# One-hot row lists of a mixture-of-experts kernel: eight assignments per VectorE instruction, token numbers multiplied in by ScalarE

## The chip, the cores and the metric

The kernel runs on one core of a Trainium2 chip. The metric is the device time of one execution in microseconds. The profile follows the five engines of the core: PE (TensorE; PEld is its weight load), DVE (VectorE), ACT (ScalarE), POOL (GpSimd) and SP (SyncE, which only issues transfers).

## The reference, cut to what matters

Two layers are computed: cross attention and a dense FFN with spline-made weights, then a state-space block and a mixture of experts. The change lies in how the rows for the experts are listed. The part of the reference that it serves is this:

```python
x2d = hidden_states.reshape(T, D)                       # T = 2048 tokens, D = 512
router_logits = x2d @ gate_kernel                       # 32 experts
routing_weights = jax.nn.softmax(router_logits, axis=-1)
routing_weights, selected_experts = jax.lax.top_k(routing_weights, TOP_K)   # TOP_K = 8
...
flat_experts = selected_experts.reshape(-1)
sort_idx = jnp.argsort(flat_experts)
token_rows = sort_idx // TOP_K
sorted_inputs = jnp.take(x2d, token_rows, axis=0)
group_sizes = jnp.bincount(flat_experts, length=NUM_EXPERTS)
w0 = jax.lax.ragged_dot(sorted_inputs, gate_proj, group_sizes)
...
```

So the 2048 x 8 assignments have to be put in order of their expert, and for each tile of 128 sorted rows the kernel needs the 128 token numbers, to gather the rows.

## The kernel before

Four blocks follow one another, with all engines meeting between two of them. `block_a` and `block_b` hold attention, FFN and state space (up to about 818 us of the profiled execution). `block_c` finishes the layer (`gate`, `add`, `normal`), computes the router's logits, chooses eight experts for each token and makes the row lists. `block_d` gathers rows by these lists, tile by tile, and runs the experts; its first gather reads `idx_all`, the last thing that `block_c` writes on VectorE (L1520).

**Making the lists.** VectorE computes in `top_place` the place of each assignment in the sorted order: 128 tokens on the partitions, 16 token tiles (`NT`), eight assignments (`TOPK`). A place is split into `sf` (its slot within a row tile, 0 to 127) and `tf` (the number of its row tile). Then a scatter is done as a product of one-hots, in the loop over `t in range(NT)` at L1498:

- VectorE writes `hot_s[t % 2][:, k, :]`, 128 columns for each assignment k: is the column the slot `sf`, times the token's number `tok` (L1503). It writes `hot_t` for k = 0 and 1: is the column at least `tf`, 170 columns (`NSTEP`, L1505).
- ScalarE writes `hot_t` for k = 2 to 7, as a Sign with the bias `neg_tf` (L1602). Because Sign gives -1 and 1 and not 0 and 1, the first two assignments use doubled token numbers (`tok[:, 1]`), and the sum is halved at the end (L1518).
- TensorE multiplies for each k `hot_s` (stationary) by `hot_t` (moving, 170 columns), all 128 products adding up in `bank[4]` (L1693). Differences of neighbouring columns give the token numbers of each row tile (L1516 to L1520).

Both one-hots have two buffers, so writing tile t waits until TensorE has used tile t - 2 (`hot_used`). In both, the columns of one assignment are neighbours in memory.

**What runs beside it.** GpSimd computes the loop's control words (`meta`) with 25 small dependent steps on one partition from L1327 on. Earlier in `block_c` it splits the first expert's weights (L1316, L1319) while VectorE runs `gate(2)` and `gate(3)` (L1441, one instruction of 2048 columns with two inputs in SBUF each). The order on each engine is the order of the code; nothing is scheduled.

Of the kernel before, what the change touches and what calls it, by code (L numbers as in the profile page):

```python
# [34 lines left out]
NE, M, TOPK = 32, 192, 8  # L35
# [13 lines left out]
NMETA = NTILE + UNROLL  # L49
NSTEP = NMETA + 2  # L50
# [1143 lines left out]
def block_c(nc, a, X, ident, kept, bank, meta, idx_all, W, y0_d, y1_d, rows_d, joined):  # L1194

    with ExitStack() as s:
        sb, sem = mem(nc, s, "C")
        st, mv, rstd, shift = sb("st", [P, LT, 6]), sb("mv", [P, LT, 2]), sb("rstd", [P, LT]), sb("shift", [P, LT])
        st2, mv2, rstd2, shift2 = sb("st2", [P, NT, 6]), sb("mv2", [P, NT, 2]), sb("rstd2", [P, NT]), sb("shift2", [P, NT])
        spare = [t[:, 2:4, :].rearrange("p s n -> p (s n)").bitcast(F32) for t in (W.gu_hi, W.gu_lo)]  # L1200
# [3 lines left out]
        HOT_END = LT * L + TOPK * NSTEP // 2  # L1204
        hot_t = [t[:, LT * L:HOT_END].bitcast(F16).rearrange("p (k n) -> p k n", k=TOPK) for t in spare]
        tau, past = (spare[0][0:NE, HOT_END + n * NMETA:HOT_END + (n + 1) * NMETA] for n in range(2))
# [7 lines left out]
        pad, tok, padm, tok_id = sb("pad", [P, D]), sb("tok", [P, 2, NT]), sb("padm", [P, NMETA]), sb("tok_id", [P, NT + PADS], I32)  # L1214
        neg_tf, twice = sb("neg_tf", [P, NT * TOPK]), sb("twice", [P, NMETA])
        guess, part = sb("guess", [P, LT]), sb("part", [P, LT])
# [7 lines left out]
        slot_i, slot_s, slot_t = (sb(n, [P, NT * TOPK], I32) for n in ("slot_i", "slot_s", "slot_t"))  # L1224
        sf, tf = sb("sf", [P, NT * TOPK]), sb("tf", [P, NT * TOPK])
        hot_s = [sb(f"hot_s{i}", [P, TOPK, P], F16) for i in range(2)]

        HOT_V = 2
        padded = sb("padded", [P, NMETA])
# [4 lines left out]
        ids_done, lgT_done = sem("ids_done"), sem("lgT_done")  # L1234
        slots_done, hot_a_done = sem("slots_done"), sem("hot_a_done")
        ld_y, ld_c = [sem(f"ld_y{i}") for i in range(2)], sem("ld_c")
# [69 lines left out]
        def _(g):  # L1306
# [53 lines left out]
        def _(v):  # L1360
# [133 lines left out]
            step(v.tensor_scalar(slot_t[:, :], slot_i[:, :], 7, None, ALU.logical_shift_right))  # L1494
            v.tensor_copy(sf[:, :], slot_s[:, :])
            step(v.tensor_copy(tf[:, :], slot_t[:, :]))
            v.tensor_scalar(neg_tf[:, :], slot_t[:, :], -1.0, 0.5, ALU.mult, ALU.add).then_inc(slots_done, 1)
            for t in range(NT):  # L1498
                if t >= 2:
                    v.wait_ge(hot_used, t - 1)  # L1500
                for k in range(TOPK):
                    j = t * TOPK + k
                    i = v.tensor_scalar(hot_s[t % 2][:, k, :], iota_s[:, :], sf[:, j:j + 1], tok[:, int(k < HOT_V), t:t + 1], ALU.is_equal, ALU.mult)  # L1503
                    if k < HOT_V:
                        v.tensor_scalar(hot_t[t % 2][:, k, :], iota_t[:, :], tf[:, j:j + 1], None, ALU.is_ge)  # L1505
                i.then_inc(hot_done, 1)
            v.wait_ge(meta_sb, 2)
# [9 lines left out]
            step(v.tensor_tensor(twice[:, :], bank[4][:, 1:NMETA + 1], padded[:, :], ALU.subtract))  # L1517
            v.tensor_scalar(halves, twice[:, :], 0.5, -1.0, ALU.mult, ALU.add)  # L1518
            step(v.scalar_tensor_tensor(out=padded[:, :], in0=twice[:, :], scalar=0.0, in1=padm[:, :], op0=ALU.is_equal, op1=ALU.mult))
# [3 lines left out]
        def _(act):  # L1523
# [621 lines left out]
```

## Time and profile before

| | |
|---|---|
| median of 3 runs | 1570.62 us (1565.63 to 1570.64) |
| span of the profiled execution | 1567.3 us |
| busy, of that span | PE 1435.0, DVE 1153.4, ACT 918.4, POOL 1062.3 us |
| `block_c` | about 818 to 930.8 us |
| loop of one-hots in it | 891.3 to 929.0 us |

The time of the profiled execution itself is not listed beside its span; the span lies among the three runs, 3.3 us under their median, so a difference worked out in the trace is put on the median. A line of the profile names the code line, the engine, the operation, output and inputs, and their shapes. `W_gu_hi` and `W_gu_lo` in the loop's rows are `hot_t`, which lies in spare room of the weight buffers; `W_d_hi` there are GpSimd's scratch rows.

### The profile page before, as it was taken

What the parts mean: (1) busy time and instruction counts of PE and PEld (TensorE: products, weight loads), DVE (VectorE), ACT (ScalarE), POOL (GpSimd) and SP (SyncE); (2) the same over time, 40 slices, a digit from 0 to 9 for tenths busy, and PEclk for the clock granted to TensorE, in tenths of its full rate; (3) what the DMA queues carried; (4) which work ended last, traced back from release to release, by engine and by line L of the source; (5) the groups of instructions that cost most, each with busy time, mean ns of one, the idle gap of its engine ahead of it and who ended that gap; (6) DMA issues with size and microseconds to landing.
All of it is one profiled execution on the core that took longest, in us unless ns stands there. A gap on an engine that the chain in (4) does not pass through costs nothing. (4 is left out here: it accounts for less than half of the span.)

```text
span 1567.3 us, 26498 instructions
## 1 busy us (share of the span) xinstructions
PE 1435.0 (92%) x6453; PEld 1073.9 (69%) x6454; DVE 1153.4 (74%) x2069; ACT 918.4 (59%) x1420; POOL 1062.3 (68%) x654
## 2 busy tenths in 40 slices
PE   6999878999999999999975559989999999999997
PEld 3444556666666666666644238878988888898886
DVE  5888897888888878888878786656666666565554
ACT  6777677666667666766646664444544444444442
POOL 2222287999999989999941235757666676666675
PEclk9999989999999999999988759999999999999999
DMA  8232557888899889988869416889998899888876
GB/s 314 96 111 98 180 132 144 179 197 205 192 196 217 186 195 178 221 188 195 176 150 336 159 31 159 193 193 209 198 200 192 191 206 201 203 186 190 189 146 118
DMA packets 106416, 283.95 MB, mean 181 GB/s; under 512 B 16641, under 2 KB 18850, under 8 KB 95090
## 3 DMA queue, kind: packets, MB, share of 16 engines
q0 software_dynamic: 43520, 155.57, 50.0%
q1 hardware_dynamic: 60322, 123.12, 26.4%
q10 hardware_dynamic: 2512, 4.52, 0.8%
q8 instruction: 27, 0.44, 0.1%
q14 instruction: 35, 0.29, 0.1%
HBM read 152.28 MB, written 135.08 MB: 183 GB/s over the span
## 5 line engine op out<-in xcount | busy, mean ns | idle before, releaser
L1156 POOL TENSOR_TENSOR B_E<-B_dtu,B_BC 128x512 f32<-128x512 f32 (+3 forms) x121 | 309.3, 2670 | 16.7 <-DMA B_BC<-bc_d 16.7
L2080 POOL DMA_INDIRECT out_x<-D_y,D_rows x144 | 243.8, 1693 | 75.4 <-issue 43.6
L889 ACT ACTIVATE bank<-B_dtv,negA 128x512 f32<-128x512 f32 x256 | 173.5, 690 | 159.8 <-DVE B_E L1024 98.1
L1024 DVE TENSOR_TENSOR_SCAN B_E<-bank,B_E 128x512 f32<-128x512 f32 x192 | 230.2, 1214 | 42.5 <-ACT bank L889 34.8
L1162 POOL TENSOR_TENSOR B_E<-B_E,B_BC 128x1536 f32<-128x1536 f32 x64 | 234.0, 3656 | 34.5 <-DVE B_E L1024 29.8
L2045 POOL DMA_INDIRECT D_rows<-rows_d,D_source x144 | 155.9, 1083 | 129.0 <-DMA out_x<-D_y,D_rows 62.3
L806 PE MATMUL bank<-B_Wd,B_inter 128*128 128x512 f32 x512 | 231.9, 606 | 9.0 <-DVE X L1011 5.3
L1906 ACT ACTIVATE D_xT_hi<-bank 128x512 fp32r<-128x512 f32 x147 | 88.1, 599 | 231.5 <-PE bank L1815 167.8
L1826 PE MATMUL bank<-W_gu_hi,D_xT_hi 128*128 x584 | 202.4, 347 | 14.5 <-ACT D_xT_hi L1906 13.9
L1968 DVE TENSOR_TENSOR D_xT_lo<-bank,D_xT_hi 128x512 fp32r<-128x512 f32 x147 | 101.3, 689 | 141.1 <-ACT D_xT_hi L1906 108.7
L1827 PE MATMUL bank<-W_gu_lo,D_xT_hi 128*128 x584 | 199.2, 341 | 0.0
L806 PEld LDWEIGHTS bank<-B_Wd,B_inter 128*128 128x128 f32 x512 | 98.3, 195 | 122.8 <-issue 102.8
L1832 PE MATMUL bank<-W_gu_hi,D_xT_lo 128*128 x584 | 131.8, 348 | 6.8 <-DVE D_xT_lo L1968 5.5
L1946 ACT ACTIVATE D_y<-bank 128x512 f32<-128x512 f32 x144 | 86.4, 600 | 83.2 <-PE bank L1899 63.6
L1826 PEld LDWEIGHTS bank<-W_gu_hi,D_xT_hi 128*128 128x128 f32 x584 | 111.1, 190 | 27.5 <-issue 22.2
L1832 PEld LDWEIGHTS bank<-W_gu_hi,D_xT_lo 128*128 128x128 f32 x584 | 103.3, 191 | 18.6 <-DVE D_xT_lo L1968 14.0
L1827 PEld LDWEIGHTS bank<-W_gu_lo,D_xT_hi 128*128 128x128 f32 x584 | 111.2, 190 | 5.5
L794 PE MATMUL bank<-hT_hi,B_Wg_hi 128*128 128x512 f32 x256 | 105.4, 412 | 7.3 <-DVE hT_lo L1064 7.3
L2032 DVE TENSOR_TENSOR W_gu_lo<-W_raw_gu,W_gu_hi x30 | 52.8, 1761 | 66.4 <-ACT W_gu_hi L1916 51.3
L795 PE MATMUL bank<-hT_lo,B_Wg_hi 128*128 128x512 f32 x256 | 100.8, 394 | 0.0
L796 PE MATMUL bank<-hT_hi,B_Wg_lo 128*128 128x512 f32 x256 | 100.3, 392 | 0.0
L1011 DVE TENSOR_TENSOR X<-bank,X 128x512 f32<-128x512 f32 x128 | 86.7, 678 | 18.2 <-PE bank L806 18.2
(327 smaller groups left out, 3263.7 us busy)
## 6 DMA issues: line engine op xcount, KB each, us to landing
y_d<-B_E POOLq DMA_DIRECT2D x64, 1024.0 KB, 10.7
B_BC<-bc_d SPq DMA_DIRECT2D x128, 256.0 KB, 6.2
W_raw_gu<-in_wgu SPq DMA_DIRECT2D x64, 384.0 KB
W_raw_d<-in_wd SPq DMA_DIRECT2D x64, 256.0 KB
X<-in_x SPq DMA_DIRECT2D x4, 1024.0 KB, 9.2
y_d<-A_du SPq DMA_DIRECT2D x4, 1024.0 KB, 4.0
dt_d<-A_dtv SPq DMA_DIRECT2D x4, 1024.0 KB, 3.9
dtu_d<-A_dtu SPq DMA_DIRECT2D x4, 1024.0 KB, 4.1
```

What stands on the lines that cost most here:

```text
L794: pe.matmul(ps[:, :], hi, h_hi, start=k == 0, stop=False)
L806: mm = pe.matmul(Yb[t % 2][:, :], chunk(jj, ch)[:, t * P:(t + 1) * P], Wd[w][:, ch, :], start=ch == 0, stop=ch == 1)
L889: act.activation(dA[m % 2][:, :], dtv[:, c, :], ACT.Exp, scale=negA[:, c, n:n + 1]).then_inc(dA_done, 1)
L1024: v.tensor_tensor_scan(state, dA[m % 2][:, :], E[:, s % NR, c, :], 0.0, ALU.mult, ALU.add).then_inc(s_done, 1)
L1156: g.tensor_tensor(E[:, s % NR, c:end, :], dtu[:, at:at + end - c, :], spread(BC[op % NBC][:, :], end - c), ALU.mult).then_inc(dbu_done, 1)
L1162: g.tensor_tensor(E[:, s % NR, 0:NW, :], E[:, s % NR, 0:NW, :], spread(BC[op % NBC][:, :], NW), ALU.mult).then_inc(prod_done, 1)
L1826: pe.matmul(ps, *operands(k, xT_hi, W.gu_hi), start=k == 0, stop=False)
L1827: pe.matmul(ps, *operands(k, xT_hi, W.gu_lo), start=False, stop=False)
L1832: mm = pe.matmul(ps, *operands(k, xT_lo, W.gu_hi), start=False, stop=k == KC - 1)
L1968: v.tensor_tensor(xT_lo[i % 2][:, :], pT[:, :], xT_hi[i % 2][:, :], ALU.subtract).then_inc(xT_sb, 1)
L2045: g.indirect_dma_start(rows[i], None, rows_d[:, :], bass.IndirectOffsetOnAxis(ap=source[i // HALF][:, i % HALF:i % HALF + 1].bitcast(U32), ...
L2080: g.indirect_dma_start(a["out"], bass.IndirectOffsetOnAxis(ap=rows[i][:, ROW - 1:ROW].bitcast(U32), axis=0), ysb[:, i, :], None, compute_o ...
```

## The change

The two one-hots of a token tile are laid out with the assignment innermost (`[P, n, k]`), and each is made by one VectorE instruction for all eight assignments: `is_equal` over 128 x 8 = 1024 columns and `is_ge` over 170 x 8 = 1360 columns, both with two fp16 inputs in SBUF. One input is a wide copy of the column numbers, each repeated eight times (`wide_s`, `wide_t`); the other is the eight values of `sf` or `tf`, read again for each column number. GpSimd makes the wide copies ahead of its weight split. ScalarE no longer makes tiles; it multiplies the slots by the token numbers, 1024 columns at once, from the new buffers `same` into `hot_s`. TensorE now reads both operands with a step of eight elements, 16 bytes. The doubling, the halving and `neg_tf` go.

```diff
-        hot_t = [t[:, LT * L:HOT_END].bitcast(F16).rearrange("p (k n) -> p k n", k=TOPK) for t in spare]
+        HOT_V = TOPK
+        hot_t = [t[:, LT * L:HOT_END].bitcast(F16) for t in spare]
+        hot_tv = [t[:, 0:HOT_V * NSTEP].rearrange("p (n k) -> p n k", k=HOT_V) for t in hot_t]
...
-        sf, tf = sb("sf", [P, NT * TOPK]), sb("tf", [P, NT * TOPK])
-        hot_s = [sb(f"hot_s{i}", [P, TOPK, P], F16) for i in range(2)]
-
-        HOT_V = 2
+        sf, tf = (sb(n, [P, NT, TOPK], F16) for n in ("sf", "tf"))
+        hot_s = [sb(f"hot_s{i}", [P, P, TOPK], F16) for i in range(2)]
+        free = [z[i].rearrange("p t l -> p (t l)").bitcast(F16) for i in range(2)]
+        wide_s = free[0][:, 0:P * TOPK].rearrange("p (n k) -> p n k", k=TOPK)
+        wide_t = free[0][:, P * TOPK:P * TOPK + NSTEP * HOT_V].rearrange("p (n k) -> p n k", k=HOT_V)
+        same = [free[1][:, i * P * TOPK:(i + 1) * P * TOPK].rearrange("p (n k) -> p n k", k=TOPK) for i in range(2)]
...
             g.wait_ge(x2_done, LT + 1)
+            g.tensor_copy(wide_s[:, :, :], each(iota_s[:, :], P, TOPK))
+            g.tensor_copy(wide_t[:, :, :], each(iota_t[:, :], NSTEP, HOT_V)).then_inc(ids_done, 1)
             g.tensor_tensor(W.slot(W.gu_lo, 0), W.slot(W.raw_gu, 0), W.slot(W.gu_hi, 0), ALU.subtract).then_inc(W.gu_split, 1)
...
-            v.tensor_scalar(neg_tf[:, :], slot_t[:, :], -1.0, 0.5, ALU.mult, ALU.add).then_inc(slots_done, 1)
+            v.wait_ge(ids_done, 2)
...
             for t in range(NT):
                 if t >= 2:
+                    v.wait_ge(hot_a_done, t - 1)
+                v.tensor_tensor(same[t % 2][:, :, :], wide_s[:, :, :], over(sf[:, t, :], P), ALU.is_equal).then_inc(same_done, 1)
+                if t >= 2:
                     v.wait_ge(hot_used, t - 1)
-                for k in range(TOPK):
-                    j = t * TOPK + k
-                    i = v.tensor_scalar(hot_s[t % 2][:, k, :], iota_s[:, :], sf[:, j:j + 1], tok[:, int(k < HOT_V), t:t + 1], ALU.is_equal, ALU.mult)
-                    if k < HOT_V:
-                        v.tensor_scalar(hot_t[t % 2][:, k, :], iota_t[:, :], tf[:, j:j + 1], None, ALU.is_ge)
-                i.then_inc(hot_done, 1)
+                v.tensor_tensor(hot_tv[t % 2], wide_t[:, :, :], over(tf[:, t, :], NSTEP), ALU.is_ge).then_inc(hot_done, 1)
...
-            v.tensor_scalar(halves, twice[:, :], 0.5, -1.0, ALU.mult, ALU.add)
+            v.tensor_scalar(halves, twice[:, :], -1.0, None, ALU.add)
...
-            act.wait_ge(slots_done, 1)
             for t in range(NT):
                 if t >= 2:
                     act.wait_ge(hot_used, t - 1)
-                for k in range(HOT_V, TOPK):
-                    j = t * TOPK + k
-                    i = act.activation(hot_t[t % 2][:, k, :], iota_t[:, :], ACT.Sign, bias=neg_tf[:, j:j + 1])
-                i.then_inc(hot_a_done, 1)
+                act.wait_ge(same_done, t + 1)
+                act.activation(hot_s[t % 2][:, :, :], same[t % 2][:, :, :], ACT.Copy, scale=tok[:, 0, t:t + 1]).then_inc(hot_a_done, 1)
...
-                    mm = pe.matmul(bank[4][:, 0:NSTEP], hot_s[t % 2][:, k, :], hot_t[t % 2][:, k, :],
+                    mm = pe.matmul(bank[4][:, 0:NSTEP], hot_s[t % 2][:, :, k], hot_tv[t % 2][:, :, k],
```

On VectorE the loop begins so before the change:

```order
L1496 CAST C_tf<-C_slot_t 128x128
L1497 TENSOR_SCALAR C_neg_tf<-C_slot_t 128x128
L1503 TENSOR_SCALAR C_hot_s<-C_iota_s,C_sf,C_tok 128x128
L1505 TENSOR_SCALAR W_gu_hi<-C_iota_t,C_tf 128x170
L1503 TENSOR_SCALAR C_hot_s<-C_iota_s,C_sf,C_tok 128x128
L1505 TENSOR_SCALAR W_gu_hi<-C_iota_t,C_tf 128x170
L1503 TENSOR_SCALAR C_hot_s<-C_iota_s,C_sf,C_tok 128x128 x7
L1505 TENSOR_SCALAR W_gu_lo<-C_iota_t,C_tf 128x170
```

And so after it, where `C_z` is the room of the buffers `wide_s`, `wide_t` and `same`:

```order
L1503 TENSOR_SCALAR C_slot_t<-C_slot_i 128x128
L1504 CAST C_sf<-C_slot_s 128x128
L1505 CAST C_tf<-C_slot_t 128x128
L1514 TENSOR_TENSOR C_z<-C_z,C_sf 128x1024
L1517 TENSOR_TENSOR W_gu_hi<-C_z,C_tf 128x1360
L1514 TENSOR_TENSOR C_z<-C_z,C_sf 128x1024
L1517 TENSOR_TENSOR W_gu_lo<-C_z,C_tf 128x1360
```

Ten instructions per token tile have become two, and the two are wide. On GpSimd, between the copy of the token numbers and the metadata steps, before:

```order
L1311 DMA y_d<-y_d 128x2048
L1313 COPY C_share<-C_tok_id 128x20
L1316 TENSOR_TENSOR W_gu_lo<-W_raw_gu,W_gu_hi 128x1536
L1319 TENSOR_TENSOR W_d_lo<-W_raw_d,W_d_hi 128x1024
L1327 TENSOR_TENSOR W_d_hi<-W_gu_lo,W_d_hi 1x168
```

And after:

```order
L1317 COPY C_share<-C_tok_id 128x20
L1323 COPY C_z<-C_iota_s 128x1024
L1324 COPY C_z<-C_iota_t 128x1360
L1325 TENSOR_TENSOR W_gu_lo<-W_raw_gu,W_gu_hi 128x1536
L1328 TENSOR_TENSOR W_d_lo<-W_raw_d,W_d_hi 128x1024
L1336 TENSOR_TENSOR W_d_hi<-W_gu_lo,W_d_hi 1x168
```

Two copies stand ahead of the weight split now.

## Rows read from the trace of the kernel before

**Rows 1.** Timeline, end of the loop and of `block_c`: start us, us, engine, line

```profile
927.49 0.23 DVE L1508 CAST W_d_hi<-W_d_hi 1x168 int32<-1x168 f32 x1
927.70 1.32 PE L1693 MATMUL bank<-W_gu_lo,C_hot_s 128*128 128x170 f16 x8 [0.82 <-DVE C_hot_s L1503]
...
929.12 0.33 DVE L1516 COPY C_padded<-bank 128x168 f32<-128x168 f32 x1
...
930.38 0.33 DVE L1520 TENSOR_TENSOR idx_all<-C_place,C_padded 128x168 int32<-128x168 f32 x1
```

**Rows 2.** Windows of the loop: stretch, its us, busy us of each engine, PEclk

```profile
889.00:907.00 18.00, 7.17 (x45) 5.54 (x46) 17.86 (x79) 14.60 (x44) 15.30 (x25) 0.50 0.19 71
907.00:927.50 20.50, 12.52 (x77) 9.18 (x75) 20.50 (x98) 18.91 (x55) 0.00 (x0) 0.50 0.00 0
```

**Rows 3.** Waits from 889 to 931 us: us in total, times, longest

```profile
PE bank L1693 <- DVE C_hot_s L1503: 19.1, 16, 4.8
```

**Rows 4.** Timeline, first slots, and starts of PE on a tile

```profile
891.16 0.23 DVE L1497 TENSOR_SCALAR C_neg_tf<-C_slot_t 128x128 f32<-128x128 int32 x1
...
893.73 1.29 PE L1693 MATMUL bank<-W_gu_hi,C_hot_s 128*128 128x170 f16 x8 [4.79 <-DVE C_hot_s L1503]
...
908.51 1.32 PE L1693 MATMUL bank<-W_gu_hi,C_hot_s 128*128 128x170 f16 x8 [0.82 <-DVE C_hot_s L1503]
...
910.64 1.31 PE L1693 MATMUL bank<-W_gu_lo,C_hot_s 128*128 128x170 f16 x8 [0.81 <-DVE C_hot_s L1503]
```

**Rows 5.** Groups from 889 to 931 us: busy us, mean ns of one

```profile
L1693 PE MATMUL bank<-W_gu_hi,C_hot_s 128*128 128x170 f16 x64 | 10.5, 344 | 11.5 <-DVE C_hot_s L1503 11.5
```

**Rows 6.** Timeline, VectorE with two float32 inputs

```profile
827.39 2.29 DVE L1441 TENSOR_TENSOR C_z<-W_gu_lo,C_z 128x2048 f32<-128x2048 f32 x1
829.60 2.48 DVE L1394 TENSOR_TENSOR X<-bank,X 128x512 f32<-128x512 f32 x4
```

**Rows 7.** Timeline, ScalarE: two widths of Copy, and one with two pointers

```profile
832.57 1.49 ACT L1526 ACTIVATE W_gu_hi<-W_raw_gu 128x1536 fp32r<-128x1536 f32 x1 [1.66 <-DMA W_raw_d<-in_wd]
...
833.96 0.61 ACT L1716 ACTIVATE W_d_hi<-W_raw_d 128x512 fp32r<-128x512 f32 x1
...
843.40 2.94 ACT L1547 ACTIVATE C_row<-X,C_shift,C_rstd 128x512 f32<-128x512 f32 x4 [6.67 <-DVE C_shift L1411]
```

**Rows 8.** Timeline, GpSimd's L543: `A_table` read by neighbours

```profile
37.14 1.27 POOL L543 TENSOR_TENSOR A_taps<-A_taps,A_table 128x512 f32<-128x512 f32 x1 [6.92 <-DMA A_dtu<-in_powers]
```

**Rows 9.** The same line two instructions later: `A_table` read four floats apart

```profile
39.60 1.58 POOL L543 TENSOR_TENSOR A_taps<-A_taps,A_table 128x512 f32<-128x512 f32 x1
```

**Rows 10.** Timeline, PE with 384 float32r columns in neighbouring words

```profile
945.26 0.34 PE L1827 MATMUL bank<-W_gu_lo,D_xT_hi 128*128 x1
945.43 0.86 PE L1832 MATMUL bank<-W_gu_hi,D_xT_lo 128*128 x4
```

**Rows 11.** Timeline, GpSimd and VectorE at `gate(2)`

```profile
837.52 3.41 POOL L1316 TENSOR_TENSOR W_gu_lo<-W_raw_gu,W_gu_hi 128x1536 fp32r<-128x1536 f32 x1
840.00 3.08 DVE L1441 TENSOR_TENSOR W_d_lo<-W_gu_hi,W_d_lo 128x2048 f32<-128x2048 f32 x1 [2.55 <-DMA W_gu_hi<-y_d]
...
847.10 2.36 POOL L1319 TENSOR_TENSOR W_d_lo<-W_raw_d,W_d_hi 128x1024 fp32r<-128x1024 f32 x1 [6.17 <-DVE X L1394]
```

**Rows 12.** Timeline, start of `block_d`: VectorE and GpSimd

```profile
931.17 1.75 DVE L1971 TENSOR_TENSOR W_gu_lo<-W_raw_gu,W_gu_hi 128x1536 fp32r<-128x1536 f32 x1
...
931.73 2.18 POOL L2049 DMA_INDIRECT D_rows<-rows_d,idx_all  x1 [24.84 <-POOLq L1196]
932.84 1.22 DVE L1972 TENSOR_TENSOR W_d_lo<-W_raw_d,W_d_hi 128x1024 fp32r<-128x1024 f32 x1
934.22 0.98 POOL L2049 DMA_INDIRECT D_rows<-rows_d,idx_all  x1 [0.30 <-issue]
```

**Rows 13.** Timeline, first and last step of GpSimd's metadata

```profile
889.54 0.53 POOL L1327 TENSOR_TENSOR W_d_hi<-W_gu_lo,W_d_hi 1x168 f32<-1x168 f32 x1 [40.08 <-ACT W_d_hi L1595]
...
906.12 0.77 POOL L1356 TENSOR_SCALAR meta<-W_d_hi 1x168 int32<-1x168 f32 x1
```

More of the change, by code:

```diff
@@ L1214, in block_c @@
         pad, tok, padm, tok_id = sb("pad", [P, D]), sb("tok", [P, 2, NT]), sb("padm", [P, NMETA]), sb("tok_id", [P, NT + PADS], I32)
-        neg_tf, twice = sb("neg_tf", [P, NT * TOPK]), sb("twice", [P, NMETA])
+        twice = sb("twice", [P, NMETA])
         guess, part = sb("guess", [P, LT]), sb("part", [P, LT])
@@ L1234, in block_c @@
         ids_done, lgT_done = sem("ids_done"), sem("lgT_done")
-        slots_done, hot_a_done = sem("slots_done"), sem("hot_a_done")
+        hot_a_done, same_done = (sem(n) for n in ("hot_a_done", "same_done"))
         ld_y, ld_c = [sem(f"ld_y{i}") for i in range(2)], sem("ld_c")
@@ L1313, in _, with each @@
             g.tensor_copy(share[:, :, NE:NE + 1].bitcast(I32), tok_id[:, :].rearrange("p (t o) -> p t o", o=1)).then_inc(ids_done, 1)
+            def each(t, n, k):
+                return t.rearrange("p (n o) -> p n o", o=1).broadcast_to([P, n, k])
             g.wait_ge(W.gu_hi_done, 1)
             g.wait_ge(x2_done, LT + 1)
+            g.tensor_copy(wide_s[:, :, :], each(iota_s[:, :], P, TOPK))
+            g.tensor_copy(wide_t[:, :, :], each(iota_t[:, :], NSTEP, HOT_V)).then_inc(ids_done, 1)
             g.tensor_tensor(W.slot(W.gu_lo, 0), W.slot(W.raw_gu, 0), W.slot(W.gu_hi, 0), ALU.subtract).then_inc(W.gu_split, 1)
@@ L1494, in _, with over @@
             step(v.tensor_scalar(slot_t[:, :], slot_i[:, :], 7, None, ALU.logical_shift_right))
-            v.tensor_copy(sf[:, :], slot_s[:, :])
-            step(v.tensor_copy(tf[:, :], slot_t[:, :]))
-            v.tensor_scalar(neg_tf[:, :], slot_t[:, :], -1.0, 0.5, ALU.mult, ALU.add).then_inc(slots_done, 1)
+            v.tensor_copy(sf[:, :, :].rearrange("p t k -> p (t k)"), slot_s[:, :])
+            step(v.tensor_copy(tf[:, :, :].rearrange("p t k -> p (t k)"), slot_t[:, :]))
+            v.wait_ge(ids_done, 2)
+            def over(t, n):
+                return t.rearrange("p (o k) -> p o k", o=1).broadcast_to([P, n, t.shape[-1]])
             for t in range(NT):
                 if t >= 2:
+                    v.wait_ge(hot_a_done, t - 1)
+                v.tensor_tensor(same[t % 2][:, :, :], wide_s[:, :, :], over(sf[:, t, :], P), ALU.is_equal).then_inc(same_done, 1)
+                if t >= 2:
                     v.wait_ge(hot_used, t - 1)
-                for k in range(TOPK):
-                    j = t * TOPK + k
-                    i = v.tensor_scalar(hot_s[t % 2][:, k, :], iota_s[:, :], sf[:, j:j + 1], tok[:, int(k < HOT_V), t:t + 1], ALU.is_equal, ALU.mult)
-                    if k < HOT_V:
-                        v.tensor_scalar(hot_t[t % 2][:, k, :], iota_t[:, :], tf[:, j:j + 1], None, ALU.is_ge)
-                i.then_inc(hot_done, 1)
+                v.tensor_tensor(hot_tv[t % 2], wide_t[:, :, :], over(tf[:, t, :], NSTEP), ALU.is_ge).then_inc(hot_done, 1)
             v.wait_ge(meta_sb, 2)
```

## The prediction, made before the changed kernel ran

> **What bounds the kernel now.** The change touches one stretch, so I looked first for where it lies: the timeline puts the loop of one-hots between 891.3 and 929.0 us, 38 of 1567 us. Then I asked what its end holds up. VectorE's last reads of `bank[4]` start 0.1 us after TensorE's last product, the list `idx_all` is the last instruction of the block, and the next block starts 0.3 us behind it [rows 1]. Block D opens with gathers that need the list [rows 12], and its weight loads start only behind those, so a microsecond won or lost in this loop should move everything after it. The reader is to see that no transfer and no other engine ends later here: GpSimd's metadata chain is done at 906.9 us [rows 13].
>
> Next, what sets the loop's pace. In the windows VectorE is busy all 20.50 of 20.50 us, ScalarE 18.9, TensorE 12.5 [rows 2], and TensorE waits for `hot_s` of VectorE in 16 of 16 tiles, 19.1 us in all [rows 3]. So VectorE is the bound. From 910.64 to 927.70 us TensorE starts eight tiles, 2.13 us each; from 893.73 to 908.51 us six tiles, 2.46 us each [rows 1, 4]. The slower ones are those beside GpSimd's 25 steps, which take 17.4 us [rows 13], 0.69 us each, 3.5 to a tile: VectorE loses 0.33 us per tile, or 0.1 us per GpSimd step.
>
> TensorE works at a granted clock of 0.50, the 1.2 GHz level [rows 2]. Eight products take 1.32 us, one alone 0.344 [rows 1, 5], so they follow each other at (1.32 - 0.344) / 7 = 0.139 us, or 0.82 ns for each of 170 columns. A tile costs it 8 x 0.139 = 1.11 us and 0.2 us of latency.
>
> **Part 1, VectorE.** Removed: eight L1503 and two L1505 per tile, and L1497; the loop's first instruction can start where L1497 does now, at 891.16 us [rows 4]. Added per tile: one instruction of 1024 columns, one of 1360. Two float32 inputs go at one column per 1.04 ns and 0.08 us per instruction: 2048 columns, start to start, are 829.60 - 827.39 = 2.21 us, and four of 512 take 2.48 [rows 6]. At that rate a tile is 1.15 + 1.50 = 2.64 us, which is more than today's 2.13. The inputs are now fp16; were they read in pairs, it is 0.61 + 0.79 = 1.40 us. No row has two 2-byte inputs on VectorE. The two bounds are 1.40 and 2.64; I take 1.40, since the instructions of the loop now, also fp16, go faster than one column per 1.04 ns (ten instructions and 1364 columns in 2.13 us, fixed costs included [rows 4]). The other bound is a rival.
>
> The Trainium skill, "VectorE: DVE Perf Modes", section "The perf-mode tier table", lists `tensor_tensor` on bf16 in SBUF at twice the rate of fp32, and "Vector Engine (DVE) Microarchitecture Reference", section 5.1, has that hold also where a row is read again and again. By it the tile is 1.40 us, without it 2.64.
>
> **Part 2, ScalarE.** Six Sign instructions per tile become one Copy of 1024 columns. Copy takes 1.49 us for 1536 and 0.61 for 512 columns, 0.86 ns a column, and pointers add about 0.1 us (four with two pointers: 2.94 us) [rows 7]. So 0.61 + 0.44 + 0.1 = 1.15 us, less than a tile on VectorE. But it now stands in a row: `is_equal`, Copy, products. For the first tile that is 891.16 + 0.69 + 1.15 + 0.1 of semaphores = 893.1 us for TensorE's start, against 893.73 now. A ring Copy, products, next but one Copy costs 1.15 + 1.32 + 0.2 = 2.7 us per two tiles, under 2 x 1.40, so it isn't the pace as long as TensorE keeps its 1.32.
>
> **Part 3, TensorE.** Still 128 products, but both operands are read with a step of 16 bytes. Nothing in the trace has TensorE reading so. The bounds for a column:
> - 0.82 ns, no cost at all (the loop now).
> - 0.82 + 0.61 = 1.43 ns. GpSimd's L543 exists in two forms that differ in this step alone: `A_table` read by neighbours takes 1.27 us [rows 8], read four floats (16 bytes) apart 1.58 us [rows 9], 0.31 us for 512 elements.
> - 1.81 ns. TensorE's float32r products of 384 columns follow each other at (0.86 - 0.34) / 3 = 0.173 us [rows 10]; that is 96 pieces of 16 bytes, 1.81 ns each. If a piece is what it fetches at a time, and that is its fastest, a 16-byte step costs a piece per column.
> - 3.1 ns, the whole time of one element in the strided L543 (1.58 us / 512), as the far end.
>
> I take 1.5: the row with just this step, moved a little towards the row of TensorE itself. Then a product is 0.255 us, a tile 2.04, more than VectorE's 1.40: **TensorE becomes the bound**. 16 x 2.04 + 0.2 = 32.8 us from 893.1 ends at 925.9, against 929.02 now [rows 1]: **-3.1 us**. The weight loads have 128 columns with the same step against 170 and stay under the products.
>
> The Trainium skill speaks on both sides. "SBUF — State Buffer", section "Specifications (TRN2)", asks for at least two hits in each 16-byte line for full bandwidth, which a step of 16 bytes never has; under "Door 1: The DMA port swizzle" the same page lets one stride for free up to 8 bf16 elements, which is this step. By the first the cost is real, by the second TensorE stays at 1.32 us per tile and the first rival below holds.
>
> **Part 4, GpSimd's two copies.** They write 2384 columns ahead of its weight split L1316, beginning at about 837.6 us. Bounds: L1316 with two inputs costs 3.41 us for 1536, 2.2 ns a column [rows 11], so 5.3 us; half of that, with one input, 2.6 us. They end between 840.2 and 842.9. There `gate(2)` on VectorE starts at 840.00; it takes 3.08 us, where 2.29 is its time alone [rows 6, 11], because L1316 runs until 840.93. The other direction shows at 931.73, where GpSimd takes 2.18 us and not 0.98 while VectorE's pair instructions run [rows 12]: whichever runs holds the other until it ends. So `gate(2)` ends at 842.5 if it slips in behind short copies (-0.6), at 845.2 behind long ones (+2.1), at 845.9 if L1316 gets in first (+2.8). VectorE is nearly gapless after it, so this counts. L1316 comes later and its first reader is the load of expert 2, far behind; L1319 waits for `x2_done` anyway until 847.1. I take **+0.5 us**, nearer to the short copies.
>
> **Part 5, the rest.** The halving goes but its instruction stays. The new wait `ids_done` is met 45 us early. `hot_a_done` ahead of `is_equal` is met when Copy of t - 2 is done. 0 us.
>
> Sum: -3.1 + 0.5 = -2.6 us. On the median of 1570.62 that is **1568.0 us**. With 1.43 to 1.81 ns for a column this forecast's own range is 1566.5 to 1575.
>
> **Rival A, the step is free (or TensorE's clock rises and hides it).** VectorE sets the pace: 891.16 + 16 x 1.40 + 25 x 0.1 for GpSimd's steps = 916.0 us; TensorE ends at 917.7 and the block 11.3 us earlier. Against all of it speaks GpSimd: each of its 25 steps may now wait behind an instruction of 0.61 or 0.79 us; with half of 0.7 each the metadata ends at 915.7, with all of it at 924.4, later than VectorE's end at 919.4, and 6.3 us stay of the gain. 1559.3 to 1564.8, most likely 1560.6. The busy share of TensorE now, 12.5 of 20.5 us, left the clock low [rows 2]; a denser loop might raise it, which speaks for this rival.
>
> **Rival B, slower: the step costs much more.** The place is the same 21,760 columns. The change breaks even when they take what the loop has now, 929.02 - 893.1 - 0.2 = 35.7 us: **1.64 ns a column**. It is 0.5% slower from 2.0 ns. At 2.4, midway between 1.81 and 3.1, the loop lasts 52.4 us: +16.5 + 0.5, 1587.6 us. For it: if both operands, each with the step, share one way of reading. Against it: GpSimd, also with two streams, pays 0.61.
>
> **Rival C, slower: VectorE takes no pairs.** The change then doesn't do what it is made for. 891.16 + 42.3 + 2.5 = 935.9, TensorE 1.4 us later, 937.3: +8.3 + 0.5, 1579.4 us. Decides if a column costs more than 0.85 ns on VectorE.
>
> **Chances.** Forecast 0.45; A 0.30; B 0.12; C 0.08; the rest 0.05, collisions at `gate(2)` or a metadata chain that eats the gain, all within half a per cent. Half a per cent, 7.85 us, is about what a measurement of this kernel can tell from no change. A is over it in four fifths of its cases (0.24), the forecast where the column costs under 1.3 ns (0.03): faster 0.27. Slower: B and most of C, 0.18. Within: 0.55. The range: down to A's best case, 1558.5, and up over C, 1581; B and small remainders stay out.
>
> **What would show it.** TensorE's group L1693: eight products in 2.0 us, with an idle time before them near nothing, confirm part 3; 1.3 us or less is A, 3 us and more is B. VectorE's two groups: 0.69 and 0.87 us are pairs, 1.22 and 1.57 are not. GpSimd's metadata should end by 921 us and its two copies last 2.6 us; `gate(2)` should end by 843.6. The forecast is wrong if the step costs TensorE nothing, and also if the loop's gain doesn't reappear in the span.

## The result, and the profile after

The changed kernel takes 1573.84 us (median of 22 runs, 1566.77 to 1581.50), the kernel before beside it 1567.42 us (22 runs, 1557.97 to 1574.01). The ratio is 1.0044, 95% interval 1.0029 to 1.0060, and a second comparison gave 1.0044 again (1.0022 to 1.0067): **0.44% or 6.9 us slower**, where 2.6 us faster was forecast. The ratios are estimates over all runs and differ a little from the quotients of the medians, here 1.0041. The profiled execution took 1576.29 us, its span 1574.5.

The loop's second half on the windows view (stretch, its us, busy us of PE, PEld, DVE, ACT, POOL, then PEclk), against [rows 2]:

```profile
889.00:907.00 18.00, 12.64 (x42) 5.76 (x42) 15.23 (x39) 7.38 (x8) 13.43 (x18) 0.50 0.22 75
907.00:927.50 20.50, 20.50 (x68) 9.72 (x67) 12.78 (x17) 9.19 (x8) 6.09 (x8) 0.50 0.00 0
```

TensorE has no gap left, VectorE went from 20.50 to 12.78 us and ScalarE from 18.9 to 9.2. TensorE's granted clock is still 0.50: working without a pause did not raise it. The groups (busy us, mean ns of one, idle before) and the waits of the loop, against [rows 3, 5]:

```profile
L1701 PE MATMUL bank<-W_gu_hi,C_hot_s 128*128 128x170 f16 x64 | 21.0, 485 | 4.2 <-ACT C_hot_s L1611 4.2
L1611 ACT ACTIVATE C_hot_s<-C_z,C_tok 128x1024 f16<-128x1024 f16 x16 | 18.4, 1149 | 20.9 <-PE bank L1701 18.0 <-DVE C_z L1514 2.9
L1514 DVE TENSOR_TENSOR C_z<-C_z,C_sf 128x1024 f16<-128x1024 f16 x16 | 12.6, 787 | 0.0
L1517 DVE TENSOR_TENSOR W_gu_lo<-C_z,C_tf 128x1360 f16<-128x1360 f16 x8 | 7.3, 916 | 5.9 <-PE bank L1701 5.9
```

The waits have turned round: ScalarE waits for TensorE 18.0 us and VectorE 11.5, TensorE for ScalarE only once. On the timeline the pace and the end of the loop, against [rows 1, 4]:

```profile
893.73 0.69 DVE L1514 TENSOR_TENSOR C_z<-C_z,C_sf 128x1024 f16<-128x1024 f16 x1
...
905.52 2.63 PE L1701 MATMUL bank<-W_gu_hi,C_hot_s 128*128 128x170 f16 x8
907.97 2.62 PE L1701 MATMUL bank<-W_gu_lo,C_hot_s 128*128 128x170 f16 x8
...
932.40 2.62 PE L1701 MATMUL bank<-W_gu_lo,C_hot_s 128*128 128x170 f16 x8
935.13 0.33 DVE L1527 COPY C_padded<-bank 128x168 f32<-128x168 f32 x1 [2.68 <-PE bank L1701]
...
936.39 0.33 DVE L1531 TENSOR_TENSOR idx_all<-C_place,C_padded 128x168 int32<-128x168 f32 x1
```

A tile is (907.97 - 905.52) = 2.45 us, a product (2.62 - 0.485) / 7 = 0.305 us, **1.80 ns a column**. And where GpSimd's copies meet `gate(2)`, GpSimd's rows and then VectorE's, against [rows 11] (L1325 and L1450 are L1316 and L1441 of before):

```profile
836.56 1.03 POOL L1323 COPY C_z<-C_iota_s 128x1024 f16<-128x1024 f16 x1
837.54 1.32 POOL L1324 COPY C_z<-C_iota_t 128x1360 f16<-128x1360 f16 x1
838.82 5.47 POOL L1325 TENSOR_TENSOR W_gu_lo<-W_raw_gu,W_gu_hi 128x1536 fp32r<-128x1536 f32 x1
...
838.57 2.42 DVE L1450 TENSOR_TENSOR W_d_lo<-W_gu_hi,W_d_lo 128x2048 f32<-128x2048 f32 x1 [2.04 <-DMA W_gu_hi<-y_d]
840.92 0.17 DVE L1419 RECIPROCAL C_rstd<-C_rstd 128x4 f32<-128x4 f32 x1
841.12 3.19 DVE L1420 SCALAR_TENSOR_TENSOR C_shift<-C_mv,C_rstd 128x4 f32<-128x4 f32 x1
844.23 2.46 DVE L1408 BATCH_NORM_STATS2 C_st<-X 128x6 f32<-128x512 f32 x4
```

`gate(2)` slips in behind the short copies and ends early, as hoped. But L1325 has waited for it, gets in behind it, and L1420 on VectorE, an instruction of 0.16 us in the kernel before (there L1411), takes 3.19 us.

To compare traces that drift against each other, I cut `block_c` of each into three stretches on VectorE: from the block's first statistics to those behind `gate(2)`; from there to the loop's first instruction (in before, L1497); from there to `idx_all`. Each length runs from start to start, in us; each ratio is against before measured beside it:

| kernel | to behind gate(2) | to the loop | loop to idx_all | sum | ratio, 95% interval |
|---|---|---|---|---|---|
| before | 25.06 | 47.88 | 39.22 | 112.16 | |
| before, second trace | 25.14 | 49.50 | 39.21 | 113.85 | |
| changed | 26.91 | 49.50 | 42.66 | 119.07 | 1.0044, 1.0029 to 1.0060 |
| changed, second trace | 27.26 | 49.37 | 42.66 | 119.29 | 1.0044, 1.0022 to 1.0067 |
| copies late | 25.08 | 49.49 | 42.65 | 117.22 | 1.0008, 0.9984 to 1.0031 |
| step of 8 bytes | | | | | 0.9958, 0.9931 to 0.9984 |
| 8 bytes, copies late | 25.03 | 49.48 | 29.67 | 104.18 | 0.9945, 0.9919 to 0.9971 |
| the same again | 25.02 | 47.85 | 29.68 | 102.55 | 0.9945, 0.9926 to 0.9964 |
| 4 bytes, copies late | 25.04 | 47.86 | 29.25 | 102.15 | 0.9938, 0.9917 to 0.9958 |
| moving operand near | 27.30 | 47.85 | 40.28 | 115.43 | 1.0030, 0.9998 to 1.0062 |
| weights near | 27.27 | 49.45 | 43.43 | 120.15 | |

The loop costs +3.4 us, `gate(2)` +1.8 to 2.2. The middle stretch has two lengths, 1.6 us apart, taken up below. What follows `idx_all` can't be compared in single traces: from its start to the end of the span it is 636.9 and 644.5 us in the two traces of before, 638.1 and 630.6 us in the two of the changed kernel. That the block's loss comes back in the whole time rests on the ratios.

### The profile page after: what moved, and what is told of

It is laid out like the page before. It is cut to its first block and busy times, and to the rows that moved or that the text cites. A ratio compares the mean times of both kernels' runs of the same rounds, so it can differ in the third digit from the quotient of the medians.

```text
span 1574.5 us, 26306 instructions
## 1 busy us (share of the span) xinstructions
PE 1454.5 (92%) x6453; PEld 1079.9 (69%) x6454; DVE 1145.5 (73%) x1940; ACT 902.4 (57%) x1340; POOL 1063.7 (68%) x656
## 5 line engine op out<-in xcount | busy, mean ns | idle before, releaser
L2088 POOL DMA_INDIRECT out_x<-D_y,D_rows x144 | 237.7, 1651 | 84.3 <-issue 48.4
L1162 POOL TENSOR_TENSOR B_E<-B_E,B_BC 128x1536 f32<-128x1536 f32 x64 | 232.4, 3632 | 33.4 <-DVE B_E L1024 27.3
L794 PE MATMUL bank<-hT_hi,B_Wu_hi 128*128 128x512 f32 x256 | 99.8, 390 | 0.0
```

What stands on the lines that cost most here:

```text
L794: pe.matmul(ps[:, :], hi, h_hi, start=k == 0, stop=False)
L1162: g.tensor_tensor(E[:, s % NR, 0:NW, :], E[:, s % NR, 0:NW, :], spread(BC[op % NBC][:, :], NW), ALU.mult).then_inc(prod_done, 1)
L2088: g.indirect_dma_start(a["out"], bass.IndirectOffsetOnAxis(ap=rows[i][:, ROW - 1:ROW].bitcast(U32), axis=0), ysb[:, i, :], None, compute_o ...
```

## The experiments

**What a step costs TensorE.** Products of zeros in the kernel before, six groups. `spaced(n)` reads every n-th fp16 value as the moving operand, `far` is a stationary operand with a step of eight:

```diff
+            def spaced(n):
+                cols = halfs.rearrange("p (m n) -> p n m", n=n)
+                return cols[:, 0:2, 0:128] if n == 8 else cols[:, 0, 0:256]
...
+                near, far = before[:, :], halfs.rearrange("p (m n) -> p n m", n=8)[:, 0, :]
+                for i in range(16):
+                    pe.matmul(bank[5][:, 0:256], near, halfs[:, 0:256], start=True, stop=True)
+                for i in range(12):
+                    pe.matmul(bank[5][:, 0:256], near, spaced(2), start=True, stop=True)
...
+                for i in range(12):
+                    pe.matmul(bank[5][:, 0:256], far, spaced(8), start=True, stop=True)
```

> The kernel before with 76 products of zeros added twice, at the start of the router's logits and in the loop of one-hots ahead of tile 8; their sums go to a bank that is written over, so they change times alone. Each has 256 fp16 columns: 16 with both operands contiguous, 12 each with the moving operand at a step of 4, 8 and 16 bytes, 12 with the stationary alone at 16 bytes, 12 with both at 16. Theory 1 (16-byte pieces, one per 1.8 ns): 0.82, 0.82 and 0.9 ns a column for contiguous, 4 and 8 bytes, 1.8 ns at 16 bytes, that is 0.21, 0.21, 0.23 and 0.46 us a product; the stationary alone at 16 bytes costs 128 x 1.8 = 0.23 us for its load, hidden or nearly so under the product. Theory 2 (any step costs a whole fetch per element): 1.8 ns at every step. Theory 3 (the weight load is what became slow, and the products wait for it): the moving operand alone costs nothing at any step, the stationary alone gives 0.3 us a product as in the changed kernel. If the granted clock is higher at one of the two places, a cost in ns that stays the same is memory's, one that halves is TensorE's own.

PE's timeline at the first place (start, us of the group, line; in the order of the expectation):

```profile
857.69 1.92 PE L1670 MATMUL bank<-C_pad,C_before 128*128 128x256 f16 x16
859.45 1.52 PE L1672 MATMUL bank<-C_pad,C_before 128*128 128x256 f16 x12
860.81 2.88 PE L1674 MATMUL bank<-C_pad,C_before 128*128 128x256 f16 x12
863.51 5.60 PE L1676 MATMUL bank<-C_pad,C_before 128*128 128x256 f16 x12
868.93 2.74 PE L1678 MATMUL bank<-C_pad 128*128 128x256 f16 x12
871.47 5.68 PE L1680 MATMUL bank<-C_pad 128*128 128x256 f16 x12
```

The windows of the fourth group and of the fifth (PEclk is the third column from the end):

```profile
863.50:868.50 5.00, 5.00 (x13) 1.30 (x12) 0.00 (x0) 0.00 (x0) 0.00 (x0) 0.97 0.03 11
868.50:871.30 2.80, 2.80 (x14) 1.98 (x13) 0.00 (x0) 0.00 (x0) 0.00 (x0) 0.50 0.00 0
```

Start to start, a moving column costs 0.43 ns contiguous, 0.44 at 4 bytes, 0.88 at 8 and 1.77 at 16 (2.70, 5.42 us for twelve products of 256 columns). The stationary operand alone at 16 bytes gives 0.83 ns (2.54 us for twelve), what contiguous products cost at this clock [rows 1]; at the high clock it was not measured. Theory 1 holds and theory 3 falls: the moving operand pays, the weight load stays under the product. At a clock of 0.97 here and 0.50 in the changed loop 16 bytes cost the same, 1.77 and 1.80 ns, so this cost does not follow TensorE's clock; that it lies in fetching the operand is inferred from this. The second place gave the same durations at 8 and 16 bytes (2.88 and 5.60 us).

**Is it a piece of 16 bytes?**

```diff
+                    pe.matmul(bank[5][:, 0:256], before[:, :], spaced(3), start=True, stop=True)
...
+                    pe.matmul(bank[5][:, 0:256], before[:, :], spaced(32), start=True, stop=True)
```

> The kernel before with 60 products of zeros added at each of the two places of the first probe (their sums are written over): a contiguous stationary operand, 256 moving fp16 columns, 12 products each at a step of 2, 6, 12, 32 and 64 bytes. The first probe gave 0.44, 0.88 and 1.77 ns a column at 4, 8 and 16 bytes. Theory 1 (pieces of 16 bytes, each fetched once): 0.66 and 1.33 ns at 6 and 12 bytes, and 1.77 ns again at 32 and 64 bytes, since a column can't cost more than a piece of its own. Theory 2 (the operand is read through, every byte between the columns too, at 9 bytes per ns): 0.66 and 1.33 ns at 6 and 12 bytes, 3.5 ns at 32 and 7.1 ns at 64. Theory 3 (a step that divides 16 is special): 6 and 12 bytes cost 1.77 ns as well.

```profile
859.90 2.22 PE L1673 MATMUL bank<-C_pad,C_before 128*128 128x256 f16 x12
861.96 4.24 PE L1675 MATMUL bank<-C_pad,C_before 128*128 128x256 f16 x12
866.02 5.71 PE L1677 MATMUL bank<-C_pad,C_before 128*128 128x256 f16 x12
871.55 5.35 PE L1679 MATMUL bank<-C_pad,C_before 128*128 128x256 f16 x12
876.73 3.60 PE L1627 MATMUL bank<-ident,C_row 128*128 128x128 f32 x15
```

Start to start, 6 bytes cost 0.67 ns a column, 12 bytes 1.32, 32 bytes 1.80, 64 bytes 1.69. The cost grows with the step up to 16 bytes and stays there: that fits pieces of 16 bytes at 1.7 to 1.8 ns each, of which a column needs at most one. Theories 2 and 3 fall. And the cost is no surcharge on TensorE's own pace: at 16 bytes a column takes 1.77 ns where a contiguous one takes 0.43 and 1.80 where it takes 0.82. The slower of the two paces counts, not their sum.

**One operand near at a time, in the kernel itself.** First `hot_t` as before:

```diff
-        hot_tv = [t[:, 0:HOT_V * NSTEP].rearrange("p (n k) -> p n k", k=HOT_V) for t in hot_t]
+        hot_tv = [t[:, 0:HOT_V * NSTEP].rearrange("p (k n) -> p k n", k=HOT_V) for t in hot_t]
...
-                v.tensor_tensor(hot_tv[t % 2], wide_t[:, :, :], over(tf[:, t, :], NSTEP), ALU.is_ge).then_inc(hot_done, 1)
+                v.tensor_tensor(hot_tv[t % 2], wide_t[:, :, :], tf[:, t, :].rearrange("p (k o) -> p k o", o=1).broadcast_to([P, HOT_V, NSTEP]), ALU.is_ge).then_inc(hot_done, 1)
...
-                    mm = pe.matmul(bank[4][:, 0:NSTEP], hot_s[t % 2][:, :, k], hot_tv[t % 2][:, :, k],
+                    mm = pe.matmul(bank[4][:, 0:NSTEP], hot_s[t % 2][:, :, k], hot_tv[t % 2][:, k, :],
```

> The changed kernel with hot_t alone laid out as before, the columns of one assignment neighbours: TensorE's moving operand is contiguous, its stationary operand keeps the 16-byte step. VectorE's is_ge then reads each value of tf 170 times in a row. If the moving operand alone carries the cost of the step: eight products in 1.3 to 1.4 us for 2.62, 0.82 ns a column; the loop is then VectorE's. If VectorE takes such reads in pairs, is_ge stays at 0.87 us, the loop takes 28 us for 41 and the kernel is 12 us under the changed one, 4 to 6 us under the kernel before; if not, is_ge takes 1.50 us (1.04 ns a column), a tile 2.2 us and more beside GpSimd, the loop 38 to 40 us, and the kernel 1 to 3 us under the changed one, 4 to 6 us over the kernel before. If the stationary operand carries the cost, TensorE stays at 2.44 us per tile and nothing changes.

A tile late in the loop:

```profile
923.75 1.56 DVE L1517 TENSOR_TENSOR W_gu_hi<-C_z,C_tf 128x1360 f16<-128x1360 f16 x1
...
925.24 0.68 DVE L1514 TENSOR_TENSOR C_z<-C_z,C_sf 128x1024 f16<-128x1024 f16 x1
925.37 1.36 PE L1701 MATMUL bank<-W_gu_hi,C_hot_s 128*128 128x170 f16 x8 [0.73 <-DVE W_gu_hi L1517]
```

TensorE is back at 1.36 us, so the moving operand carried the cost. But `is_ge` lost its pairs, 1.56 us and not 0.87: a value read 170 times in a row is no pair. The time is 4.7 us over before (-0.3 to +9.8), as expected for this case. Now the reverse, `hot_s` near:

```diff
-        hot_s = [sb(f"hot_s{i}", [P, P, TOPK], F16) for i in range(2)]
+        hot_s = [sb(f"hot_s{i}", [P, TOPK, P], F16) for i in range(2)]
...
-                act.activation(hot_s[t % 2][:, :, :], same[t % 2][:, :, :], ACT.Copy, scale=tok[:, 0, t:t + 1]).then_inc(hot_a_done, 1)
+                act.activation(hot_s[t % 2][:, :, :], same[t % 2].rearrange("p n k -> p k n"), ACT.Copy, scale=tok[:, 0, t:t + 1]).then_inc(hot_a_done, 1)
...
-                    mm = pe.matmul(bank[4][:, 0:NSTEP], hot_s[t % 2][:, :, k], hot_tv[t % 2][:, :, k],
+                    mm = pe.matmul(bank[4][:, 0:NSTEP], hot_s[t % 2][:, k, :], hot_tv[t % 2][:, :, k],
```

> The reverse of the run with a contiguous moving operand: ScalarE writes hot_s with each assignment's slots as neighbours and reads same with the 16-byte step, so that TensorE's stationary operand is contiguous and the moving one keeps its step. If the moving operand alone carries the cost, TensorE stays at 2.44 us per tile (1.80 ns a column), with shorter weight loads (0.10 for 0.15 us) that buy nothing, and the time is the changed kernel's within 1 us, unless ScalarE pays for its own step: up to 1.8 ns a column would make Copy 1.15 into 1.9 us, still under TensorE's 2.44. If the stationary operand carries it, eight products take 1.3 us.

```profile
L1611 ACT ACTIVATE C_hot_s<-C_z,C_tok 128x1024 f16<-128x1024 f16 x16 | 33.9, 2128 | 7.1 <-PE bank L1701 4.7 <-DVE C_z L1514 2.4
L1701 PE MATMUL bank<-W_gu_lo,C_hot_s 128*128 128x170 f16 x64 | 20.5, 476 | 0.0
L1701 PEld LDWEIGHTS bank<-W_gu_lo,C_hot_s 128*128 128x128 f16 x64 | 7.2, 120 | 12.1 <-issue 12.1
```

TensorE's products keep their 0.48 us, so the moving operand's step is the cost; the time, 1579.11 us, is of one run. ScalarE pays for the step too: its Copy went from 1.15 to 2.13 us, 0.96 ns more for each of 1024 columns, a little over the 1.9 expected. The first Copy delays TensorE's start by this one microsecond, and the loop is 0.8 us longer.

**The copies' place.** They move behind both weight splits, L1325 and L1328.

```diff
-            g.tensor_copy(wide_s[:, :, :], each(iota_s[:, :], P, TOPK))
-            g.tensor_copy(wide_t[:, :, :], each(iota_t[:, :], NSTEP, HOT_V)).then_inc(ids_done, 1)
...
+            g.tensor_copy(wide_s[:, :, :], each(iota_s[:, :], P, TOPK))
+            g.tensor_copy(wide_t[:, :, :], each(iota_t[:, :], NSTEP, HOT_V)).then_inc(ids_done, 1)
```

> The changed kernel with GpSimd's two wide copies moved behind its second weight split, some 12 us later, where VectorE's weight-free work runs and nothing waits for GpSimd. Theory 1 (the copies cost because they push the weight split L1325 out of the time in which gate(2) runs and into the time of the small VectorE instruction L1420, which then takes 3.19 us for 0.16): L1420 is back at 0.2 us, the stretch from GpSimd's share copy to the loop is 3.0 to 3.5 us shorter, the loop stays at 2.44 us per tile, and the kernel is 3 to 3.5 us faster than the changed one, level with the kernel before or 3.4 us over it. Theory 2 (the 3.5 us before the loop are chance of the one execution, the loop alone makes the difference): no change against the changed kernel, +6.9 us on the kernel before. Theory 3 (the copies collide wherever they stand): two or three us are lost at the new place and the sum is as before.

```profile
836.18 3.04 DVE L1450 TENSOR_TENSOR W_d_lo<-W_gu_hi,W_d_lo 128x2048 f32<-128x2048 f32 x1 [2.62 <-DMA W_gu_hi<-y_d]
839.14 0.16 DVE L1419 RECIPROCAL C_rstd<-C_rstd 128x4 f32<-128x4 f32 x1
839.34 0.16 DVE L1420 SCALAR_TENSOR_TENSOR C_shift<-C_mv,C_rstd 128x4 f32<-128x4 f32 x1
...
845.54 3.10 POOL L1327 COPY C_z<-C_iota_s 128x1024 f16<-128x1024 f16 x1
```

L1420 is at 0.16 us and the first stretch back at 25.08. All three traces with late copies and a shorter step show that too; all four with early copies have 26.9 to 27.3. So the cause stands, but with 1.8 to 2.2 us and not the 3.0 to 3.5 that I expected: the rest of those lay in the middle stretch, which did not move. The copies still meet VectorE at their new place: beside `gate(3)` the first takes 3.10 us for 1.03, and the next L1420 0.79 us. But that costs nothing further on, the middle stretch stays at 49.49 us, so theory 3 falls. The time is 1.3 us over before (-2.5 to +4.9), where the changed kernel is 6.9 over; this agrees with the trace, but is too wide to tell 1.8 us from 3.5. The order of the collision varies: in the two kernels with one operand near, early copies too, L1325 was first and `gate(2)` itself took 5.4 to 5.5 us, for the same loss.

**Is the middle stretch the change's?**

> The kernel before, unchanged, for a second trace of it. The loop starts 1.6 us later behind gate(2) in all three traces of changed kernels than in the trace of before, since TensorE's sixteen transposes and the logits of the second row tile take 7.2 us there and 5.6 us in before, at a lower granted clock. If that comes with the change, the 5.6 us are here again; if it is the chance of where the clock's fall meets them, this trace may show either, and 7.2 us here would prove it. Time: that of before.

In the first trace of before, and in this one:

```profile
851.67 1.97 PE L1616 MATMUL bank<-ident,W_d_hi 128*128 128x128 f32 x16 [2.49 <-DVE W_d_hi L1441]
853.57 3.62 PE L1635 MATMUL bank<-C_hT,C_gk 128*32 128x512 f32 x8
```

```profile
849.23 2.45 PE L1616 MATMUL bank<-ident,W_d_hi 128*128 128x128 f32 x16 [2.78 <-DVE W_d_hi L1441]
851.61 4.77 PE L1635 MATMUL bank<-C_hT,C_gk 128*32 128x512 f32 x8
```

Both lengths occur in the same kernel, 5.6 and 7.2 us, so it is not simply the change's. Whether the change makes the long one more frequent stays open: with the code of before up to there it was long in one of four traces, with early copies in three of four, with late ones in two of four. That could be worth some 0.8 us, or nothing.

**A shorter step.** Four assignments innermost, then two, with and without the late copies:

```diff
-        hot_tv = [t[:, 0:HOT_V * NSTEP].rearrange("p (n k) -> p n k", k=HOT_V) for t in hot_t]
+        KI = 4
+        hot_tv = [t[:, 0:HOT_V * NSTEP].rearrange("p (h n k) -> p h n k", n=NSTEP, k=KI) for t in hot_t]
...
-                    mm = pe.matmul(bank[4][:, 0:NSTEP], hot_s[t % 2][:, :, k], hot_tv[t % 2][:, :, k],
+                    mm = pe.matmul(bank[4][:, 0:NSTEP], hot_s[t % 2][:, k // KI, :, k % KI], hot_tv[t % 2][:, k // KI, :, k % KI],
```

> The changed kernel with the assignments innermost by four and not by eight, so that TensorE reads both operands with a step of 8 bytes; VectorE's and ScalarE's instructions keep their 1024 and 1360 columns, GpSimd's copies have half of theirs. Theory 1 (TensorE fetches a row in pieces of 16 bytes, one per 1.8 ns at this clock): 0.9 ns a column, eight products in some 1.3 us instead of 2.62, TensorE no longer the bound, a tile every 1.56 to 1.75 us by VectorE; the loop ends 11 to 14 us sooner, and the kernel is about 12 us under the changed one, 5 us under the kernel before. Theory 2 (any step over one element costs the same, each element is fetched by itself): still 1.80 ns a column, 2.44 us per tile, the kernel within 1 us of the changed one.

> Both edits together: assignments innermost by four (step of 8 bytes), and GpSimd's copies behind its second weight split. If the piece of 16 bytes and the collision at L1420 are both right, the gains add up: about 1558 to 1560 us, 8 to 10 us under the kernel before and 15 us under the changed one. If only the collision is right, some 3 us over the kernel before; if only the piece, 5 us under it; if neither, 7 us over it.

The first gave 0.9958 (its profiled execution took 2740.3 us and is not read), the second 0.9945: 6.6 and 8.6 us under before, where 5 and 8 to 10 were expected. What the late copies add is within the noise here. The second's loop, beside GpSimd's steps and after them:

```profile
905.44 1.14 DVE L1521 TENSOR_TENSOR W_gu_hi<-C_z,C_tf 128x1360 f16<-128x1360 f16 x1
906.90 1.39 PE L1705 MATMUL bank<-W_gu_hi,C_hot_s 128*128 128x170 f16 x8 [0.25 <-ACT C_hot_s L1615]
...
913.02 0.68 DVE L1518 TENSOR_TENSOR C_z<-C_z,C_sf 128x1024 f16<-128x1024 f16 x1
913.63 0.87 DVE L1521 TENSOR_TENSOR W_gu_lo<-C_z,C_tf 128x1360 f16<-128x1360 f16 x1
914.42 0.68 DVE L1518 TENSOR_TENSOR C_z<-C_z,C_sf 128x1024 f16<-128x1024 f16 x1
```

Eight products take 1.39 us, and VectorE is the bound: 914.42 - 913.02 = 1.40 us per tile alone, up to 1.85 beside GpSimd's steps. The loop fell from 42.66 to 29.67 us.

> The changed kernel, unchanged, on the chip that also runs the two kernels with shorter steps. The first instruction of its block to the last (idx_all) took 119.1 us in its trace, 113.9 in the second trace of before: +5.2 us, of which 3.4 are the loop (TensorE at 1.80 ns a column) and 1.8 the collision at gate(2). If these two are all, the ratio is 1.0033; if the time also moves elsewhere, it stays at the 1.0044 measured first.

> The kernel with the 8-byte step and late copies again: its block took 104.2 us, 9.7 under the second trace of before. By that 9.7 us faster than before, ratio 0.9938, and 14.9 under the changed kernel.

> The same with the assignments innermost by two: a step of 4 bytes on TensorE, runs of two on VectorE. TensorE, at 0.44 ns a column when its clock is high and 0.82 when low, pays nothing at all; it was no longer the bound with 8 bytes, so it buys only the tail, 0.1 us. What decides is VectorE: if it takes runs of two, read again and again, in pairs, its instructions stay at 0.69 and 0.87 us and the kernel is level with the 8-byte one within 1 us; if the run must be longer, as is_ge's single repeated values gave 1.56 us, they take 1.2 and 1.57 us, a tile 2.7 us and more, and the kernel is 8 to 13 us over the kernel before.

On one chip the changed kernel is at 1.0044, the 8-byte step at 0.9945, the 4-byte step at 0.9938: medians of 1575.24, 1559.64 and 1557.73 us, where before takes 1566.37. For the changed kernel 1.0033 was expected if the loop and `gate(2)` are all; the interval, 1.0022 to 1.0067, holds that as well as the 1.0044, so it doesn't decide. For the 8-byte step 0.9938 was expected, inside its interval. With runs of two VectorE keeps its 0.68 and 0.85 us, so they are read in pairs. The two versions can't be told apart; both beat before and the changed kernel.

## Why the prediction was wrong

- **What bounds the kernel: right.** TensorE's end and the list's end set the block's end. Against the trace of before with the same middle stretch, the blocks of the two 8-byte traces are 9.6 and 9.7 us shorter, and 8.6 us are measured.
- **Part 1, VectorE: right.** Pairs, 0.69 and 0.87 us where 1.40 for both was taken; rival C falls.
- **Part 2, ScalarE: right.** 1.149 us for 1.15, and TensorE starts 2.02 us after the first `is_equal`, 1.94 predicted. But that instruction started 893.73 - 844.23 = 49.50 us behind the statistics, not 47.88 as L1497 in the trace of before: the middle stretch.
- **Part 3, TensorE: this step failed.** That the step costs time and makes TensorE the bound was right, the value not. Between 1.43 and 1.81 ns I took 1.5, "the row with just this step, moved a little towards the row of TensorE itself". Measured: 1.80, the value of [rows 10]. The step in [rows 9] is GpSimd's, which needs 2.5 ns for an element anyway (1.27 us for 512), so that part of a fetch may lie under its work, which no run here tested. The lower bound, 0.82 + 0.61, also laid GpSimd's surcharge on TensorE's own pace, and the runs show no such sum: 1.77 ns at the high clock, 1.80 at the low. Nor did [rows 10] show the limit of reading; that it met 1.80 is partly luck. Its products ran at a granted clock of 1.00, and 0.173 us for 384 columns is 0.45 ns a column, close to the 0.43 of contiguous fp16 columns at that clock. So it may be TensorE's own pace, and is then only a ceiling for the time of a piece, as the prediction's "if that is its fastest" allows. The probes alone show the 1.77 to 1.80.

  On the 21,760 columns the 0.3 ns are 6.5 us: -3.1 becomes the +3.4 seen. The break-even of 1.64 ns was right, and lay between the two values, so the choice decided the sign.

  The Trainium skill, "SBUF — State Buffer", section "Specifications (TRN2)", asks for two hits in each 16-byte line. This case's traces agree that a step of 16 bytes pays (1.80 ns) and show that two hits are nearly enough only at the low clock (1.39 us for 1.32 per eight products): at the high one 8 bytes cost 0.88 ns for 0.43. The same page, under "Door 1: The DMA port swizzle", lets one stride for free up to 8 bf16 elements; for the moving operand with fp16, also two bytes each, the measured 1.80 ns refute that.
- **Part 4, GpSimd's copies: sized wrong.** They took 1.03 + 1.32 us for 2.6 to 5.3, about 1 ns a column. `gate(2)` slipped in behind the short copies and ended by 843.6, as asked for. That case was priced at -0.6 because I had left out what comes next: the weight split then follows `gate(2)` and holds VectorE's next instruction with two inputs. Measured +1.8 to 2.2 us, inside the -0.6 to +2.8 given; +0.5 was taken. The case priced at +2.8, L1316 first, came in the two kernels with one operand near, and cost 2.2.
- **Part 5: right** in its terms. The metadata chain ends at 913.7, before the 921 that was asked for, and nobody waits for it.
- **Rival A's remark on the clock: wrong for this kernel.** TensorE was busy in all 20.50 us, and the clock stayed at 0.50. With the 8-byte step and late copies, busy in 11.02 of 13.00 us from 907 us on, it was 0.63 on average.

The two misses are 6.5 and 1.5 us: -2.6 becomes +5.4. 6.9 was measured (4.5 to 9.4), so 1.5 us aren't placed; they lie within the interval, and the two lengths of the middle stretch are of that size. The time fell inside the range, but on the other side of before; its 0.44% lies in the case of less than half a per cent either way, which had been given 0.55. One slip in the range: its lower end, 1558.5, is called rival A's best case, which was worked out as 1559.3; nothing hangs on it.

## What to carry to other kernels

Before an operand is laid out for the engine that writes it, work out what the engine that reads it pays. For TensorE's moving operand here that is some 0.11 ns for each byte from one column to the next, up to 16 bytes, and never less than the column's own 0.43 or 0.82 ns. When two values for an unknown cost straddle the break-even, as 1.43 and 1.81 ns did, the middle is no forecast of the sign: a short probe with products of zeros settled it here. A row of another engine carries over badly, since a part of its cost may lie under slower work, and a row of the same engine bounds the cost only if that row was not itself limited by something else. Interleaving by four or two instead of eight gave VectorE the same wide instructions and TensorE nearly its old pace.

## What the runs showed of the hardware

- TensorE's moving operand: 0.43, 0.44, 0.67, 0.88, 1.32, 1.77, 1.80 and 1.69 ns a column at steps of 2, 4, 6, 8, 12, 16, 32 and 64 bytes. Those up to 16 bytes are at a granted clock of 0.91 to 1.00, 32 and 64 bytes at 0.50; at 16 bytes both levels were measured, 1.77 and 1.80 ns. The stationary operand's step of 16 bytes costs nothing that the products show at 0.50 (0.83 ns a column).
- TensorE's granted clock fell to 0.50 (1.2 GHz) behind products of the 16-byte step although it was busy in all 5.00 us of them.
- VectorE reads two fp16 inputs in pairs when the repeated one comes in runs of two, four or eight (0.68, 0.85 to 0.87 us), and not when single values repeat (1.56 us). The Trainium skill, "VectorE: DVE Perf Modes", section "Mode 2×_1P — pack two bf16 into one 32-bit read", wants neighbours in memory for a pair, and both cases agree.
- An instruction of 4 columns with two inputs on VectorE waited 3 us behind GpSimd's (3.19 us for 0.16), while the RECIPROCAL ahead of it, with one input, did not (0.17 us).
